# First attention logits of a graph network: every source lookup by TensorE, the sums by GpSimd

## The chip, the core and the metric

The kernel runs on one core of a Trainium2 chip. The metric is device time in microseconds for one launch, as a median over runs. The engines are TensorE (PE in the profile; PEld is its weight load), VectorE (DVE), ScalarE (ACT), GpSimd (POOL) and SyncE (SP). They run side by side and meet only at semaphores. GpSimd also issues the indirect DMAs, which fetch table rows by an index from memory.

## What is computed

Two graph attention layers, each with a residual and a layer norm, over 3125 nodes of 1024 numbers and 50000 edges. The change touches the first layer alone, and there only its logits:

```python
xp = (x @ W).reshape(N, H, C)                     # 3125 x 4 heads x 256
a_src = jnp.einsum('nhc,hc->nh', xp, att_src)     # 4 numbers a node
a_dst = jnp.einsum('nhc,hc->nh', xp, att_dst)
e = jax.nn.leaky_relu(a_src[src] + a_dst[dst], NEG_SLOPE)
m = jax.ops.segment_max(e, dst, num_segments=N)
ee = jnp.exp(e - m[dst])
z = jax.ops.segment_sum(ee, dst, num_segments=N)
out = jax.ops.segment_sum(xp[src] * (ee / z[dst])[:, :, None], dst, num_segments=N)
```

The edges are sorted by `dst`, and every node also has an edge to itself.

## The kernel before, in words

The sorted edges lie in chunks of 128, one edge on a partition: 391 chunks. The kernel walks windows of 64 destination nodes; a chunk that crosses a window's border is visited twice, so there are T = 440 steps. Four steps (U = 4) are a group, so there are NG = 110 groups of steps, and NGC = 98 groups of chunks. Five groups (GU = 5) are a unit; there are NU = 22 units.

A first block (to about 91 us of the profiled span) transposes x into `xT_all`, gets `a_src` and `a_dst` of all nodes (`a_all`), and builds the index tables. The block after it, here called the logits stage, does two things at once.

- **The product x @ W.** For each of 24 node tiles (the 25th is finished later) TensorE does 16 float32 matmuls of 512 columns (`products`, L990; a float32 matmul shows as two records in the trace). VectorE adds the bias and stores to `xp_st` (`evict_xp`, L1123), and SP writes it out. PSUM banks 0 to 3 hold two tiles.
- **The logits.** For each group TensorE fetches the destination part with a one-hot matrix of the local node number (`look_up`, L966, 4 matmuls), which VectorE has made by a comparison (`onehots`, L1072). VectorE adds the three bfloat16 parts (`reduce`, L1079). The source part `ga` comes in one of two ways. For groups 2 and 4 of each unit (`PICKS`, 38 of the 98 groups of chunks) VectorE compares the low 7 bits of the source number (`compare_sources`, L1100, and the tile number in L1103), TensorE multiplies the one-hot with the whole table (`look_up_sources`, L976, 12 matmuls of 100 columns, PSUM bank 6), and VectorE picks the right tile by a product and a sum (`pick_sources`, L1110 and L1114). For the other 60 groups (`FETCHED`) GpSimd issues four indirect DMAs each from `a_src_table` in device memory (`fetch_sources`, L165), and marks a landed group by a memset of one word (L383) that raises `s_fetched`. VectorE then adds the two parts (`logits`, L1089, 4 adds), copies the self part (L1092), and forms the slope (L1094).

The order is written out by hand, per unit. TensorE does `look_up`, in groups 1 and 3 `look_up_sources`, and then a slice of the product (4, 4, 4, 2, 2 matmuls after the five lookups). VectorE's `turn` for group g is: one-hot of g, reduction of g-1, logits of g-4 (LAG = 3). ScalarE's queue loads the rows `lt` and `low_bc`, broadcast to all partitions. `PoolGather.wait` sits between GpSimd's DMAs, and it goes two groups ahead of what has landed. When all logits are there (`s_lg`), TensorE transposes them (L1017), and the softmax scan starts. The later stages gather too: 440 rows of 4 KB for the first layer's sums, and 392 rows in the second layer's logits, all through L165.

Of the kernel before, what the change touches and what calls it, by code (L numbers as in the profile page):

```python
# [60 lines left out]
PICKS = (2, 4)  # L61
PICK_UNITS = NGC // GU
PICKED = [q for q in range(PICK_UNITS * GU) if q % GU in PICKS]
FETCHED = [q for q in range(NGC) if q not in PICKED]
NPICK = len(PICKED)
# [247 lines left out]
def gnn_kernel(nc, x, src, dst, w0, att_s, att_d, bias, rms_w, w_down, wl, wr, att1, w_up, out):  # L313
# [6 lines left out]
    as_t = nc.dram_tensor("a_src_table", (NP, H), F32, kind="Internal").ap()  # L320
# [16 lines left out]
    with top:  # L337
# [28 lines left out]
        chi = front.enter_context(nc.sbuf_tensor("chi", [P, NPICK, U], F32))  # L366
# [4 lines left out]
        s_ga = [sem(f"p1_ga{i}") for i in range(2)]  # L371
        s_fetched = sem("p1_fetched")
        EARLY = 1
        FIRST_K = 4

        def fetch_sources(pool, turns):
            gather = PoolGather(pool, N, bound)
            for p in turns:
                if p >= 2:
                    gather.wait(s_ga[p % 2], 64 * (p // 2))  # L380
                    q = FETCHED[p - 2]
                    gather.wait(s_fetched, q)
                    nc.gpsimd.memset(tick[:, q:q + 1], 0).then_inc(s_fetched, 2 if q + 1 in PICKED else 1)  # L383
                if p < len(FETCHED):
                    for c in range(FETCHED[p] * U, (FETCHED[p] + 1) * U):
                        gather.rows_of(ga[:, c, :], as_t, csrc[:, c:c + 1]).then_inc(s_ga[p % 2], 16)
            return gather
# [3 lines left out]
        with ExitStack() as ph:  # L391
# [83 lines left out]
            s_as = setup_sem("s_as")  # L475
# [74 lines left out]
            with nc.Block() as block:  # L550
                @block.gpsimd
                def _(pool):
                    pool.wait_ge(s_ct, 1)
                    pool.dma_start(edge_t.rearrange("(b p) n -> p b n", b=NB),
                                   ct[:].rearrange("p b f k -> p b (f k)")).then_inc(s_et, 16)
                    gather = PoolGather(pool, T, bound)
                    pool.wait_ge(s_ci, 1)
                    pool.wait_ge(s_et, 16)
                    for b in range(NB):
                        gather.rows_of(st[:, b, :, :].rearrange("p f k -> p (f k)"), edge_t, cii[:, b:b + 1])\  # L560
                              .then_inc(s_st, 16)
                    pool.wait_ge(s_csrc, 1)
                    pool.wait_ge(s_as, 32)
                    fetch_sources(pool, range(EARLY))

                @block.sync
                def _(sp):
# [29 lines left out]
                    as_rows = as_t.rearrange("(t p) h -> p t h", p=P)  # L597
                    with nc.allow_non_contiguous_dma(reason="four words a node"):
                        for i, tiles in enumerate((slice(0, HALF), slice(HALF, NT))):
                            sp.wait_ge(s_all, i + 1)  # L600
                            sp.dma_start(as_rows[:, tiles, :], a_all[:, tiles, 0:H]).then_inc(s_as, 16)
                    sp.wait_ge(s_et, 16)
                    sp.wait_ge(s_as, 32)
# [104 lines left out]
                def _(dve):  # L708
# [62 lines left out]
                    for n, i in enumerate(PICKS):  # L771
                        nc.vector.tensor_copy(chi[:, n::2, :], psum[:, 5, 0:PICK_UNITS * GU * U]
                                              .rearrange("p (q j) -> p q j", j=GU * U)[:, :, i * U:(i + 1) * U])
# [62 lines left out]
        with ExitStack() as ph:  # L836
# [8 lines left out]
            low_bc = sb("low_bc", [P, 2, U, P], BF16)  # L845
# [14 lines left out]
            s_low = [sem(f"p1_low{i}") for i in range(2)]  # L860
# [5 lines left out]
            s_hl = sem("p1_onehot_low")  # L866
            s_hp = sem("p1_looked_up")
# [18 lines left out]
            with nc.Block() as block:  # L886
                @block.gpsimd
                def _(pool):
                    fetch_sources(pool, range(EARLY, len(FETCHED) + 2))

# [14 lines left out]
                def _(act):  # L905
                    def load_low(u, n):
                        wait(act, s_hl, 2 * u + n - 1)
                        act.dma_start(low_bc[:, n].rearrange("p j e -> p (j e)"),
                                      low_t[bass.ds((GU * u + PICKS[n]) * U, U), :].rearrange("j e -> (j e)")
                                      .partition_broadcast(P)).then_inc(s_low[n], 16)  # L910
# [7 lines left out]
                    def unit(u, r, static):  # L918
                        for i in range(GU):
                            if i % 2 == 0 and i // 2 < 2 and static < PICK_UNITS:  # L920
                                load_low(u, i // 2)
                            load_lt(GU * u + i, i)
                    pairs(act, unit)
# [34 lines left out]
                def _(pe):  # L958
# [12 lines left out]
                    def look_up_sources(u, n):  # L971
                        pe.wait_ge(s_hl, 2 * u + n + 1)
                        wait(pe, s_hm, 2 * u + n)
                        for j in range(U):
                            for k in range(PARTS):
                                last = nc.tensor.matmul(psum[:, 6, j * NT * H:(j + 1) * NT * H], onehot_low[:, n, j, :],  # L976
                                                        as0[:, :, k, :], start=(k == 0), stop=(k == PARTS - 1))
                        last.then_inc(s_hp, 1)

                    def products(u, r, k0, k1):  # L980
                        if k0 == 0:
                            wait(pe, s_xe, u - 1)
                        for k in range(k0, k1):
                            for i in range(2):
                                if isinstance(u, int) and u == NT - 1:
                                    last = nc.tensor.matmul(
                                        psum[WN * i:WN * (i + 1), 2 * r], xT_all[:, u, k, 0:WN],
                                        w_sb[:, k, i * 512:(i + 1) * 512], start=(k == 0), stop=(k == KD - 1))
                                    continue
                                last = nc.tensor.matmul(  # L990
                                    psum[:, 2 * r + i], xT_all[:, u, k, :],
                                    w_sb[:, k, i * 512:(i + 1) * 512], start=(k == 0), stop=(k == KD - 1))
                        if k1 == KD:
                            last.then_inc(s_xp, 1)
# [7 lines left out]
                    SLICES = ((0, 2), (2, 4), (4, 6), (6, 7), (7, 8))  # L1002

                    def unit(u, r, static):
                        for i, (k0, k1) in enumerate(SLICES):
                            look_up(GU * u + i, i, (GU * r + i) % 2)
                            if i in (1, 3) and static < PICK_UNITS:
                                look_up_sources(u, i // 2)
                            products(u + 1, 1 - r, k0, k1)
# [53 lines left out]
                def _(dve):  # L1063
                    nc.vector.tensor_copy(w9[:, :, 2 * H], isfirst[:])
                    chunks = StepTiles(dve, ctab, "p1_c", U, NGC * U)
                    last_group = dve.alloc_register("p1_last")
                    group_of = dve.alloc_register("p1_last_bounded")

                    def onehots(g, i, s, m):
                        dve.wait_ge(s_lt[i], 16 * m + 16)  # L1070
# [5 lines left out]
                    def reduce(g, i, s):  # L1076
                        dve.wait_ge(s_pg, g + 1)
                        pv = psum[:, 4 + s, 0:U * PARTS * 2 * H].rearrange("p (j k n) -> p j n k", k=PARTS, n=2 * H)
                        nc.vector.tensor_reduce(out=at_dst[:, i], in_=pv, op=ALU.add, axis=AX.X).then_inc(s_at, 1)  # L1079

                    def logits(g, i, s, picks):
                        cs = chunks.load(g)
                        dve.reg_alu(last_group, chunks.regs[U - 1], 2, ALU.logical_shift_right)
                        dve.reg_alu(group_of, last_group, 0, ALU.max)
                        dve.wait_ge(s_at, g + 1)
                        wait(dve, s_hd, picks)
                        dve.wait_ge(s_fetched, dve.snap(group_of, min_val=0, max_val=NGC - 1) + 1)
                        for j in range(U):
                            last = nc.vector.tensor_tensor(esum[:, s, j], at_dst[:, i, j, 0:H],  # L1089
                                                           ga[:, bass.ds(cs[j], 1), :].rearrange("p a n -> p (a n)"), ALU.add)  # L1090
                        last.then_inc(s_es, 1)
                        nc.vector.tensor_copy(w9[:, bass.ds(g * U, U), H:2 * H], at_dst[:, i, :, H:2 * H])  # L1092
# [4 lines left out]
                    def compare_sources(u, n):  # L1097
                        dve.wait_ge(s_low[n], 16 * u + 16)
                        wait(dve, s_hp, 2 * u + n - 1)
                        nc.vector.tensor_scalar(onehot_low[:, n].rearrange("p j e -> p (j e)"),  # L1100
                                                low_bc[:, n].rearrange("p j e -> p (j e)"), pidx[:], None,
                                                ALU.is_equal).then_inc(s_hl, 1)
                        nc.vector.tensor_tensor(  # L1103
                            onehot_hi[:, n], bc(iotar[:, 0:NT].unsqueeze(1), [P, U, NT]),
                            bc(chi[:, bass.ds(2 * u + n, 1), :].rearrange("p a j -> p (a j)").unsqueeze(2), [P, U, NT]),
                            ALU.is_equal)

                    def pick_sources(u, n):
# [1228 lines left out]
```

## Time and profile before

| what | us |
|---|---|
| median of 3 runs | 2171.18 |
| lowest and highest run | 2164.91, 2173.71 |
| span of the profiled execution | 2761.9 |
| logits stage in that execution, first lookup to first transpose of the logits | 99.8 to 734.3 |
| GpSimd's last gather of `a_src` issued | 420.7 |

The profile is of one execution. It is to be read in this order: the span against the timed runs, the slices of engine activity, then the stretches 99 to 439 and 439 to 735 us apart, and inside each the list of instructions in order of time. In that list a row can stand for several instructions of one line (xN), and the bracket gives the idle time of the engine ahead of it and what ended it; "issue" means that nothing the profile shows was waited for.

### The profile page before, as it was taken

How to read it: one execution, taken by the hardware profiler on the slowest of the kernel's cores; microseconds unless marked ns; L12 is line 12 of the kernel's file. 1: busy time of each engine (PE TensorE's matmuls, PEld its weight loads, DVE VectorE, ACT ScalarE, POOL GpSimd, SP SyncE). 2: the span in 40 equal slices, each digit the busy share in tenths (PEclk: the TensorE clock that was granted, in tenths of full speed). 3: DMA queues.
4: the chain of work that ended last, by engine and by line, in shares of the span. 5: the costliest groups of instructions: out<-in, count | busy, mean ns of one | idle time of the engine just before them, and what ended most of it. 6: DMA issues, size and time to landing. Idle time of an engine off the chain costs nothing. (4 is left out here: it accounts for less than half of the span.)

```text
span 2761.9 us, 52467 instructions
## 1 busy us (share of the span) xinstructions
PE 1865.4 (68%) x11779; PEld 1216.8 (44%) x11780; DVE 1524.7 (55%) x4081; ACT 862.2 (31%) x2923; POOL 1346.7 (49%) x1446
## 2 busy tenths in 40 slices
PE   5612119999857777777774886367677676856678
PEld 4300004444434555545553775244445444545544
DVE  5301006777655555555555996254544544678878
ACT  3000000000246666656564674100000000046656
POOL 1576770000046666666663112826666666147781
PEclk9855558999979999999998998688888888979999
DMA  8201002332168888888887994556766666478857
GB/s 302 49 2 21 4 15 72 98 91 87 44 203 297 295 291 291 291 292 295 291 293 239 306 308 145 145 154 193 192 194 190 194 194 195 141 218 310 308 187 267
DMA packets 256917, 531.76 MB, mean 193 GB/s; under 512 B 50253, under 2 KB 148694, under 8 KB 256782
## 3 DMA queue, kind: packets, MB, share of 16 engines
q0 software_dynamic: 95376, 276.01, 32.0%
q1 hardware_dynamic: 124142, 220.58, 23.8%
q10 hardware_dynamic: 37296, 33.96, 5.0%
q8 instruction: 44, 0.72, 0.1%
q14 instruction: 59, 0.48, 0.1%
HBM read 441.14 MB, written 102.23 MB: 197 GB/s over the span
## 5 line engine op out<-in xcount | busy, mean ns | idle before, releaser
L165 POOL DMA_INDIRECT acc<-xl_table,csrc x392 | 401.3, 1024 | 243.7 <-issue 110.7
L1274 ACT ACTIVATE wone<-onehot,w 128x64 f32<-128x64 f32 x1760 | 433.3, 333 | 278.3 <-DVE onehot L1320 174.0
L1291 PE MATMUL banks<-w_sb,wone 128*64 128x256 f32 x2368 | 346.6, 416 | 135.1 <-DVE acc L1316 42.1
L990 PE MATMUL banks<-w_sb,acc 128*128 128x512 f32 x736 | 367.1, 637 | 36.7 <-issue 36.5
L1768 PE MATMUL banks<-xr_parts,onehot_t 128*128 x1320 | 228.3, 314 | 241.3 <-issue 186.4
L165 POOL DMA_INDIRECT w_sb<-xp_table,isrc x296 | 294.5, 995 | 171.8 <-PE banks L1294 91.5
L1808 DVE SCALAR_TENSOR_TENSOR prod<-banks,att_relu 128x1024 f32<-128x1024 f32 x110 | 134.6, 1223 | 323.2 <-ACT w L1727 238.2
L1316 DVE TENSOR_TENSOR acc<-banks,acc 128x512 f32 x440 | 304.4, 692 | 0.0
L1768 PEld LDWEIGHTS banks<-xr_parts,onehot_t 128*128 128x128 bf16 x1320 | 137.3, 104 | 343.7 <-issue 302.3
L165 POOL DMA_INDIRECT ga<-a_src_table,csrc x240 | 239.4, 998 | 94.9 <-issue 76.6
L1291 PEld LDWEIGHTS banks<-w_sb,wone 128*64 128x64 f32 x2368 | 183.1, 145 | 193.5 <-issue 83.2
L1773 PE MATMUL banks<-acc,ident 128*128 x880 | 259.1, 444 | 8.9 <-POOL tabs L1678 4.3
L1315 DVE TENSOR_TENSOR zacc<-banks,zacc 64x9 f32 x440 | 69.5, 158 | 319.0 <-PE banks L1294 198.8
L1727 ACT ACTIVATE w<-banks 128x32 f32 (+1 forms) x110 | 21.6, 197 | 664.8 <-remote 356.3
L990 PEld LDWEIGHTS banks<-w_sb,acc 128*128 128x128 f32 x736 | 137.2, 199 | 174.9 <-issue 174.8
L1773 PEld LDWEIGHTS banks<-acc,ident 128*128 128x128 f32 x880 | 186.7, 224 | 54.7 <-issue 16.0
L1079 DVE TENSOR_REDUCE at_dst<-banks 128x32 f32<-128x96 f32 x110 | 28.0, 255 | 330.9 <-remote 217.1
L1291 PE MATMUL banks<-rows_c,wone 128*64 128x256 f32 x1152 | 164.2, 414 | 63.6 <-ACT wone L1274 29.1
L926 ACT ACTIVATE zacc<-pidx 128x450 f32<-128x450 f32 x1 | 0.6, 578 | 620.1 <-DVE onehot_t L1072 620.1
L165 POOL DMA_INDIRECT rows_c<-xp_table,isrc x144 | 142.8, 992 | 89.3 <-PE banks L1294 53.7
L1918 POOL TENSOR_TENSOR msg<-rows,w 128x1536 f32<-128x1536 f32 x55 | 151.7, 2777 | 52.1 <-PE banks L1958 34.3
L1254 POOL MEMSET acc<- 128x3072 f32 x1 | 2.7, 2663 | 356.6 <-POOLq L886 356.6
(336 smaller groups left out, 2966.0 us busy)
## 6 DMA issues: line engine op xcount, KB each, us to landing
edge_rows<-acc SPq DMA_DIRECT2D x440, 130.0 KB
rows<-edge_rows SPq DMA_DIRECT2D x55, 1040.0 KB, 5.0
lt_bc<-local_dst ACTq DMA_DIRECT2D x110, 128.0 KB
lt<-local_dst ACTq DMA_DIRECT2D x110, 128.0 KB
w<-acc SPq DMA_DIRECT2D x100, 128.0 KB, 3.4
x_table<-y POOLq DMA_DIRECT2D x25, 512.0 KB, 6.2
acc<-x_table SPq DMA_DIRECT2D x25, 512.0 KB, 3.7
acc<-in_x SPq DMA_DIRECT2D x12, 1024.0 KB, 14.7
```

The lines of the kernel that those rows point to most:

```text
L165: return self.pool.indirect_dma_start(out, None, table, bass.IndirectOffsetOnAxis(ap=idx, axis=0), bounds_check=self.bound, oob_is_err=False)
L990: last = nc.tensor.matmul(psum[:, 2 * r + i], xT_all[:, u, k, :], w_sb[:, k, i * 512:(i + 1) * 512], start=(k == 0), stop=(k == KD - 1))
L1079: nc.vector.tensor_reduce(out=at_dst[:, i], in_=pv, op=ALU.add, axis=AX.X).then_inc(s_at, 1)
L1274: last = nc.scalar.activation(wone[:, s, j, h, :], onehot[:, s, j, :], ACT.Copy, scale=w9[:, bass.ds(g * U + j, 1), h:h + 1].rearrange("p ...
L1291: nc.tensor.matmul(psum[WN * a:WN * (a + 1), j, k * C:(k + 1) * C], wone[:, s, j, h, :], slots[r][:, j, h * C:(h + 1) * C], start=True, st ...
L1315: nc.vector.tensor_tensor(zv, psum[0:WN, 4 + j, 0:W9], zv, ALU.add)
L1316: nc.vector.tensor_tensor(av, psum[:, j, :], av, ALU.add).then_inc(s_acc, 1)
L1727: nc.scalar.activation(w9[:, bass.ds(g * U, U), 0:2 * H], psum[:, 4 * s2:4 * s2 + 4, HID:XRW], ACT.Copy).then_inc(s_sc, 1)
L1768: nc.tensor.matmul(psum[:, 4 * s2 + j, 0:XRW], onehot_t[:, s2, j, :], xr_parts[:, bass.ds(ds[j], 1), k, :].rearrange("p a n -> p (a n)"), ...
L1773: last = nc.tensor.matmul(psum[:, 4 * s2 + j, 0:XLW], ident[:], rows[:, bass.ds(ss[j], 1), :].rearrange("p a n -> p (a n)"), start=False, ...
L1808: nc.vector.scalar_tensor_tensor(out=prod[:, s], in0=psum[:, 4 * s:4 * s + 4, 0:HID], scalar=0.0, in1=bc(att_relu[:].unsqueeze(1), [P, U, ...
L1918: nc.gpsimd.tensor_tensor(msg[:, s, :, 0:POOL_HEADS, 0:HD], rows[:, r, :, 0:POOL_HEADS * HD].rearrange("p j (h c) -> p j h c", c=HD), bc(w ...
```

## The change

All 98 groups of chunks get their source part by `look_up_sources`, one in each group of steps; `fetch_sources`, `a_src_table`, its two stores and the marks are gone. The comparison result, the PSUM bank (6 + s) and `onehot_hi` are double buffered by s. `low_bc` is loaded for every group, five buffers deep, on the same semaphores as `lt`. The product's slices become 3, 3, 3, 3 and 4 matmuls. GpSimd runs a new loop, `sums`: the copy of the self part and the four adds; VectorE keeps only `slopes` of the logits.

```diff
-PICKS = (2, 4)
...
-    as_t = nc.dram_tensor("a_src_table", (NP, H), F32, kind="Internal").ap()
...
-        def fetch_sources(pool, turns):
...
-                    for c in range(FETCHED[p] * U, (FETCHED[p] + 1) * U):
-                        gather.rows_of(ga[:, c, :], as_t, csrc[:, c:c + 1]).then_inc(s_ga[p % 2], 16)
...
-                            sp.dma_start(as_rows[:, tiles, :], a_all[:, tiles, 0:H]).then_inc(s_as, 16)
...
-                    for n, i in enumerate(PICKS):
...
+                    nc.vector.tensor_copy(chi[:].rearrange("p q j -> p (q j)"), psum[:, 5, 0:NGC * U])
...
-                    fetch_sources(pool, range(EARLY, len(FETCHED) + 2))
+                    chunks = StepTiles(pool, ctab, "p1_c", U, NGC * U)
+
+                    def sums(g, i, s):
+                        cs = chunks.load(g)
+                        pool.wait_ge(s_at, g + 1)
+                        pool.wait_ge(s_hd, min(g + 1, NGC) if isinstance(g, int) else g + 1)
+                        wait(pool, s_lg, g - 1)
+                        nc.gpsimd.tensor_copy(w9[:, bass.ds(g * U, U), H:2 * H], at_dst[:, i, :, H:2 * H])
+                        for j in range(U):
+                            last = nc.gpsimd.tensor_tensor(esum[:, s, j], at_dst[:, i, j, 0:H],
+                                                           ga[:, bass.ds(cs[j], 1), :].rearrange("p a n -> p (a n)"), ALU.add)
+                        last.then_inc(s_es, 1)
...
                             load_lt(GU * u + i, i)
+                            if GU * static + i < NGC:
+                                load_low(GU * u + i, i)
...
+                    def look_up_sources(q, s):
+                        pe.wait_ge(s_hl, q + 1)
+                        wait(pe, s_hm, q - 1)
                         for j in range(U):
                             for k in range(PARTS):
-                                last = nc.tensor.matmul(psum[:, 6, j * NT * H:(j + 1) * NT * H], onehot_low[:, n, j, :],
+                                last = nc.tensor.matmul(psum[:, 6 + s, j * NT * H:(j + 1) * NT * H], onehot_low[:, s, j, :],
                                                         as0[:, :, k, :], start=(k == 0), stop=(k == PARTS - 1))
...
-                    SLICES = ((0, 2), (2, 4), (4, 6), (6, 7), (7, 8))
+                    SLICES = ((0, 3), (3, 6), (6, 9), (9, 12), (12, 16))
...
                     def reduce(g, i, s):
                         dve.wait_ge(s_pg, g + 1)
+                        wait(dve, s_es, g - (GU - 1))
...
-                    def logits(g, i, s, picks):
...
+                    def slopes(g, s):
                         dve.wait_ge(s_es, g + 1)
...
                         if not last:
-                            onehots(g, i, (GU * r + i) % 2, u)
...
+                            onehots(g, i, s, u)
+                        if first < NGC:
+                            compare_sources(g, i, s, u)
+                        if first >= 1 and not (last and i > 0):
+                            reduce(g - 1, (i - 1) % GU, s1)
+                        if 1 <= first <= NGC:
+                            pick_sources(g - 1, s1)
+                        if first >= 1 + LAG:
+                            slopes(g - 1 - LAG, (GU * r + i - 1 - LAG) % 2)
```

On TensorE, in the middle of a unit before, a group with a source lookup and the start of the next, which has none (`nt` is the table of destinations, `as` that of sources, ISA rows load registers):

```order
L966 MATMUL banks<-nt,onehot_t 128x24
L976 MATMUL banks<-as,onehot_low 128x100 x12
L990 MATMUL banks<-w_sb,acc 128x512 x2
L146 TENSOR_LOAD tabs
L147 ISA
L966 ISA
```

The same place now:

```order
L949 MATMUL banks<-nt,onehot_t 128x24
L959 MATMUL banks<-as,onehot_low 128x100 x12
L973 MATMUL banks<-w_sb,acc 128x512 x3
L142 TENSOR_LOAD tabs
L143 ISA
L949 ISA
```

The 12 matmuls now stand behind every lookup of destinations up to group 97, and the slice of the product behind them is 3 or 4 matmuls.

On VectorE, one turn of the second unit before, a turn without picks:

```order
L1072 TENSOR_SCALAR onehot_t<-lt_bc,pidx 128x512 [waits p1_pg,p1_lt1]
L1077 REGISTER_ALU
L1079 TENSOR_REDUCE at_dst<-banks 128x32 [waits p1_pg]
L146 ISA
L146 TENSOR_LOAD tabs
L147 ISA
L83 REGISTER_ALU [waits p1_at]
L1087 ISA [waits p1_picked]
L1089 ISA [waits p1_fetched]
L1089 TENSOR_TENSOR esum<-at_dst,ga 128x4
```

Every turn now, up to group 97 (`p1_es` is raised by GpSimd, `p1_looked_up` by TensorE):

```order
L1059 TENSOR_SCALAR onehot_t<-lt_bc,pidx 128x512 [waits p1_pg,p1_lt3]
L1077 TENSOR_SCALAR onehot_low<-low_bc,pidx 128x512 [waits p1_looked_up,p1_lt3]
L1080 ISA
L1080 TENSOR_TENSOR onehot_hi<-iotar,chi 128x100
L1067 TENSOR_REDUCE at_dst<-banks 128x32 [waits p1_es,p1_pg]
L1089 TENSOR_TENSOR picked<-banks,onehot_hi 128x400 [waits p1_looked_up,p1_picked,p1_onehot_hi]
L1093 ISA [waits p1_chosen]
L1093 TENSOR_REDUCE ga<-picked 128x16
L1071 ISA [waits p1_es]
L1071 SCALAR_TENSOR_TENSOR w<-esum 128x4x4
```

The register load, the four adds and the copy have left VectorE, and two comparisons, a product and a sum have come into each turn. On GpSimd the gathers give way to this row of work, here one group of steps:

```order
L142 TENSOR_LOAD tabs
L143 ISA
L863 COPY w<-at_dst 128x4x4
L865 ISA
L865 TENSOR_TENSOR esum<-at_dst,ga 128x4
L865 ISA
L865 TENSOR_TENSOR esum<-at_dst,ga 128x4
L865 ISA
L865 TENSOR_TENSOR esum<-at_dst,ga 128x4
L865 ISA
L865 TENSOR_TENSOR esum<-at_dst,ga 128x4
```

Before, four `L165 DMA ga<-a_src_table,csrc` and a one-word memset stood there for each of the 60 groups.

## Rows read from the trace of the kernel before

**Rows 1.** The page: span, and busy tenths of PE and GpSimd in 40 slices.

```profile
span 2761.9 us, 52467 instructions
...
PE   5612119999857777777774886367677676856678
...
POOL 1576770000046666666663112826666666147781
```

**Rows 2.** Busy us (and instructions) by stretch: PE, PEld, DVE, ACT, POOL, clock, DMA.

```profile
99.00:439.00 340.00, 88.91 (x262) 36.28 (x261) 35.23 (x141) 0.00 (x0) 235.78 (x290) 0.57 0.10 15
439.00:735.00 296.00, 294.79 (x1357) 140.95 (x1356) 203.51 (x913) 13.92 (x15) 0.00 (x0) 1.00 0.29 88
```

**Rows 3.** PE in order of time at 239 to 243 us: start, length, [idle before].

```profile
239.87 0.18 PE L966 MATMUL banks<-nt,onehot_t 128*128 x1 [1.79 <-issue]
242.68 0.18 PE L966 MATMUL banks<-nt,onehot_t 128*128 x1 [2.64 <-issue]
```

**Rows 4.** One unit of PE at 449 to 465 us, in order of time.

```profile
449.52 0.25 PE L966 MATMUL banks<-nt,onehot_t 128*128 x4
...
453.14 0.25 PE L966 MATMUL banks<-nt,onehot_t 128*128 x4
453.25 0.71 PE L976 MATMUL banks<-as,onehot_low 128*128 128x100 bf16 x12
...
457.30 0.25 PE L966 MATMUL banks<-nt,onehot_t 128*128 x4
...
465.26 0.25 PE L966 MATMUL banks<-nt,onehot_t 128*128 x4
```

**Rows 5.** GpSimd in order of time: one fetched group of four gathers, then the next.

```profile
274.77 0.99 POOL L165 DMA_INDIRECT ga<-a_src_table,csrc  x1 [0.22 <-issue]
...
279.97 1.00 POOL L165 DMA_INDIRECT ga<-a_src_table,csrc  x1 [0.21 <-issue]
```

**Rows 6.** L1808, once a group in the second layer's logits: busy us (count) by stretch.

```profile
1810.00:2360.00 550.00, 110.12 (x90) 0.86 0.68 191
2360.00:2430.00 70.00, 18.35 (x15) 0.95 0.34 102
```

**Rows 7.** GpSimd alone by L165 in three gathering stretches: busy us (count), clock, DMA.

```profile
99.90:420.00 320.10, 227.93 (x230) 0.56 0.09 12
800.00:1450.00 650.00, 403.80 (x407) 0.94 0.87 293
```

**Rows 8.** VectorE in order of time at 528 to 533 us.

```profile
528.52 0.35 DVE L1100 TENSOR_SCALAR onehot_low<-low_bc,pidx 128x512 bf16<-128x512 bf16 x1
528.79 0.25 DVE L1103 TENSOR_TENSOR onehot_hi<-iotar,chi 128x100 f32<-128x100 f32 x1
528.97 0.57 DVE L1110 TENSOR_TENSOR picked<-banks,onehot_hi 128x400 f32<-128x400 f32 x1
529.70 0.89 DVE L1114 TENSOR_REDUCE ga<-picked 128x400 f32 x1 [0.17 <-DVE picked L1110]
530.50 0.34 DVE L1072 TENSOR_SCALAR onehot_t<-lt_bc,pidx 128x512 bf16<-128x512 bf16 x1
530.76 0.25 DVE L1079 TENSOR_REDUCE at_dst<-banks 128x32 f32<-128x96 f32 x1
...
531.69 0.18 DVE L1094 SCALAR_TENSOR_TENSOR w<-esum 128x16 f32 x1
531.87 1.23 DVE L1123 TENSOR_TENSOR xp_st<-banks,bias_bc 128x1024 f32<-128x1024 f32 x1
```

**Rows 9.** GpSimd's computing instructions elsewhere in the program, in order of time.

```profile
6.00 0.19 POOL L508 CAST step<-stepi 110x4 f32<-110x4 int32 x1
...
6.87 0.30 POOL L514 CAST pidx<-tabs 128x1 f32<-128x1 int32 x1
```

**Rows 10.** The end of the logits stage in order of time.

```profile
728.84 0.55 DVE L1089 TENSOR_TENSOR esum<-at_dst,ga 128x4 f32<-128x4 f32 x4 [0.68 <-DVE at_dst L1079]
...
734.33 1.90 PE L1017 MATMUL banks<-ident,w 128*110 128x128 f32 x15 [1.21 <-DVE w L1094]
```

More of the change, by code:

```diff
@@ L888, in _, with unit @@
                 def _(pool):
-                    fetch_sources(pool, range(EARLY, len(FETCHED) + 2))
+                    chunks = StepTiles(pool, ctab, "p1_c", U, NGC * U)
[9 more added lines that the diff above has]
+                        last.then_inc(s_es, 1)
+                    def unit(u, r, static):
+                        for i in range(GU):
+                            sums(GU * u + i, i, (GU * r + i) % 2)
+                    pairs(pool, unit)
                 @block.sync
@@ L977, in look_up_sources, with halves @@
                                                         as0[:, :, k, :], start=(k == 0), stop=(k == PARTS - 1))
                         last.then_inc(s_hp, 1)
-                    def products(u, r, k0, k1):
[L981 to L994, printed above, removed]
+                    def halves(u, r, n0, n1):
+                        if n0 == 0:
+                            wait(pe, s_xe, u - 1)
+                        for n in range(n0, n1):
+                            k, i = divmod(n, 2)
+                            if isinstance(u, int) and u == NT - 1:
+                                last = nc.tensor.matmul(
+                                    psum[WN * i:WN * (i + 1), 2 * r], xT_all[:, u, k, 0:WN],
+                                    w_sb[:, k, i * 512:(i + 1) * 512], start=(k == 0), stop=(k == KD - 1))
+                                continue
+                            last = nc.tensor.matmul(
+                                psum[:, 2 * r + i], xT_all[:, u, k, :],
+                                w_sb[:, k, i * 512:(i + 1) * 512], start=(k == 0), stop=(k == KD - 1))
+                        if n1 == 2 * KD:
+                            last.then_inc(s_xp, 1)
@@ L1095, in logits, with compare_sources @@
                                                        in1=esum[:, s], op0=ALU.mult, op1=ALU.max).then_inc(s_lg, 1)
[L1097 to L1101, printed above, removed]
+                    def compare_sources(q, i, s, m):
+                        dve.wait_ge(s_lt[i], loaded(i, m))
+                        wait(dve, s_hp, q - 1)
+                        nc.vector.tensor_scalar(onehot_low[:, s].rearrange("p j e -> p (j e)"),
+                                                low_bc[:, i].rearrange("p j e -> p (j e)"), pidx[:], None,
@@ L1124, in evict_xp, with turn @@
                                                 bias_bc[:], ALU.add).then_inc(s_xe, 1)
[L1126 to L1127 removed]
+                    def turn(u, r, i, static):
+                        g, first, last = GU * u + i, GU * static + i, static == NU
+                        s, s1 = (GU * r + i) % 2, (GU * r + i - 1) % 2
                         if not last:
[L1129 to L1137 removed]
+                            onehots(g, i, s, u)
[7 more added lines that the diff above has]
+                            slopes(g - 1 - LAG, (GU * r + i - 1 - LAG) % 2)
                     def unit(u, r, static):
@@ L1156, in _ @@
                         for r in range(2):
-                            unit(2 * pair + r, r, 0)
+                            unit(2 * pair + r, r, 2)
                     for u in range(2 * (PICK_UNITS // 2), NU):
@@ L1160, in _ @@
                     for i in range(LAG + 1):
[L1161 removed]
+                        turn(NU, NU % 2, i, NU)
                         if i == 1:
```

114 lines of the change are left out of this document (29 added, 85 removed).

## Prediction, written before the run

> **What bounds the kernel now.** I read first the span against the timed runs, because they differ more than the change could move. The profiled span is 2761.9 us [rows 1], the median 2171.18 us, so 591 us of the profiled execution are in no timed run. A sum made against this profile is worth nothing before it is known whose 591 us they are. So the second view is the busy slices: the logits stage lies in slices 2 to 11 of 69 us each; in slices 3 to 6 GpSimd is at 6 or 7 tenths and PE at 1 or 2, in slices 7 to 10 PE is at 9 and GpSimd at 0 [rows 1]. Taken by itself this reads as "the gathers of a_src hold TensorE up for 340 us, take them away". The stretches say the same in sums: from 99 to 439 us PE is busy 89 of 340 us at a mean granted clock of 0.57, with 236 us of GpSimd; from 439 to 735 it is busy 295 of 296 us at full clock, with none [rows 2].
>
> The third view, instructions in order of time, speaks against that reading. Between 239 and 243 us PE runs the single matmuls of one lookup, with only a register instruction between them, and each stands 2.81 us behind the one before, idle "issue" 2.64 us [rows 3]. At 453.14 us four of the same kind fit in 0.25 us [rows 4]. No semaphore stands between these four, so a gather that isn't back can't be what they wait for. A gather can hold VectorE's logits, and through the buffers a lookup, but not the second matmul of four. Nor do the gathers come late: GpSimd's four of a group take 279.97 - 274.77 = 5.20 us [rows 5], 3 groups in 5 are fetched, so it feeds a unit of five groups each 15.6 us, and a unit of PE takes 465.26 - 449.52 = 15.74 us [rows 4]. It starts ahead of PE, and 110 groups of steps need only 98 groups of chunks. What I see there is engines slowed in their issue while small gathers are in flight, in this profiled execution.
>
> Are these stalls in the timed runs too? The bookkeeping says no. Without them the stage's 22 units would be 19 with two source lookups at 15.74 us and 3 without. A source lookup costs PE (457.30 - 453.14) - (453.14 - 449.52) = 4.16 - 3.62 = 0.54 us [rows 4], so a unit without is 15.74 - 1.08 = 14.66 us. Sum: 19 x 15.74 + 3 x 14.66 = 343 us, against 630 us in the profile (99.8 us to about 729.4): **287 us lost**. The second layer's logits, under gathers too, take 550 / 90 = 6.11 us a group and, once the gathers have ended, 70 / 15 = 4.67 us [rows 6]; 1.44 us by some 98 groups is 141 us. The gathers for the first layer's sums come each 650 / 407 = 1.60 us [rows 7] where GpSimd alone needs 1.30 [rows 5]; 0.30 by 440 is 132 us. Together 560 us, near the 591 to be explained. If the 287 us were real in timed runs, 591 us would have to come from what gives 273. So I take it that **in the timed runs the stage is bound by TensorE already**, at about 343 us, and that the gathers run hidden beside it.
>
> **The change part by part.**
>
> *TensorE.* 60 more source lookups by 0.54 us = 32.4 us, on the engine that sets the end; the matmuls of the product and the lookups of destinations are the same in number. A unit with five lookups is 14.66 + 5 x 0.54 = 17.36 us, 3.47 us a group. The new slices only spread this more evenly. Sum for the stage: 343 + 32 = 375 us.
>
> *GpSimd's gathers and the a_src_table.* 240 gathers by 1.30 us go, 312 us of GpSimd, hidden beside 343 us of TensorE: worth 0 in the timed runs. Their cover is thin. Before would be gather bound if one took over (99.8 + 343 - 8 - 92) / 236 = 1.45 us, with 92 us where the stage's gathers start, 236 of them, and some 8 us from the last landing to the stage's end. The rows give 1.30 alone and 320.1 / 230 = 1.39 with all waits [rows 5, 7]; the 1.60 of the later stage is the far bound, and there GpSimd also waits for TensorE and 4 KB rows. At 1.60 the old stage would be 35 us longer, and the change worth -3 us instead of +32. I take 1.30 to 1.39, since these are the same gathers. The two stores of a_src_table end beside VectorE's table building: 0.
>
> *VectorE.* From start to start [rows 8]: comparison 0.27, tile comparison 0.18, product 0.73, sum 0.80, one-hot 0.26, reduction 0.25, slope 0.18: 2.67 us a group, and 1.23 us of eviction a unit, 5 x 2.67 + 1.23 = 14.6 us. That fits under 17.36 us of TensorE, with 2.8 us left in a unit. Order matters as well: TensorE's next lookup needs one-hot and comparison, which stand behind product and sum of the group before. From the end of a source lookup these are 0.73 + 0.80 + 0.18 + 0.26 + 0.27 = 2.2 us, and TensorE has its slice (2.6 us), the next lookups (0.6 us) and one more slice in hand before it needs them. So no wait.
>
> *GpSimd's sums.* Five small instructions and a register load a group. None like them stands in the trace. A small conversion takes 0.19 to 0.30 us [rows 9], VectorE's gap for the same register load and waits is 0.68 us [rows 10]. 5 x 0.19 + 0.68 = 1.6 us at the low end, 5 x 0.30 + 0.68 = 2.2 us at the high one; it speaks in the end only from 3.47 us a group on. LAG of three turns, some 10 us, hides the way from VectorE to GpSimd and back. What is queued behind it: VectorE's slope, and behind that the next one-hots. 0 us.
>
> *DMAs.* low_bc is loaded 98 times instead of 38, 128 KB each: 10 loads of 128 KB in 17.4 us, 75 GB/s, five buffers ahead. 0 us. *Ends.* The first block's copy to chi is longer, +0.2 us. At the end TensorE waited 1.21 us for the last slope [rows 10]; now a slice of 4 matmuls stands behind the last lookup, and VectorE's four late logits are only four slopes: -1.2 us.
>
> Sum: +32.4 + 0.2 - 1.2 = +31.4 us, and **2171.2 + 31.4 = 2202.6 us**, 1.4% slower. Against the profile's own time the sum is another: the stage loses 630 - 343 = 287 us of stalls with the gathers and gains 31, so I expect a profiled span of about 2761.9 - 287 + 31 = 2506 us, if the stalls elsewhere stay. The profiled execution should look 256 us faster while the median is 31 us slower.
>
> **A rule of the skill.** The comparisons treat 128 x 512 bfloat16 in 0.35 us [rows 8], over one element a nanosecond on each partition, and GpSimd has computed next to nothing beside them in this stage. The Trainium skill ("SBUF — State Buffer", Who interferes with whom) says that VectorE in a two-port mode, or with two SBUF inputs against a GpSimd instruction that reads SBUF, shares a port pair with GpSimd as a lock, and the later one blocks fully. By that rule the sums given to GpSimd are paid back in part by VectorE's comparisons, and the change comes out slower yet: it is the mechanism of rival (c), which is priced below from rows. No row of this trace has small GpSimd sums beside such comparisons, so it shows neither.
>
> **The rivals.** (a) *The stalls are real*, and the gathers hold the timed runs too, wholly or in part. For it: they are long and in the trace, and the change's gain in the profile is large. Against: the bookkeeping. In full 2171 - 256 = 1915 us; at a third of it about 2107. Chance 0.13. (b) *Gathers a little slower* than in the rows: at a cadence of 1.50 us the old stage is 236 x (1.50 - 1.45) = 11 us over TensorE's sum, at 1.65 us 47 us, so the new time is 2171 + 31 - 11 = 2191 to 2171 + 31 - 47 = 2155 us. For it: 15.6 against 15.7 us a unit, and 1.60 in rows 7. Against: 1.30 stands wherever GpSimd isn't waiting. Chance 0.14: 0.03 faster, 0.08 within 0.5% of before, 0.03 slower. (c) *VectorE becomes the bound* on account of GpSimd's instructions: each of the five holds VectorE up for its own length, 5 x (0.19 to 0.30) = 0.95 to 1.5 us a group. VectorE is then at 14.6 / 5 + 0.95 = 3.87 to 4.4 us a group against TensorE's 3.47: 98 groups by 0.4 to 0.95 = 39 to 93 us more, 2242 to 2296 us. It decides from 0.55 us a group on. Chance 0.12. (d) *GpSimd is the bound*, over 3.47 us a group, through waits and register work that cost more than on VectorE; at 4 us a group 98 x 0.5 = 52 us, 2255 us. Chance 0.04.
>
> **How the numbers follow.** The forecast as worked out, 2190 to 2215 us, has 0.57. With it, of rival (b) what lies above 2165 us, 0.12, and of (c) and (d) the cheaper part, 0.10, make 0.79; so the range is **2165 to 2260 us**. About 0.5% (11 us) is what a measurement of this kernel can tell from no change. Slower by more: 0.57 + 0.12 + 0.04 + 0.03 = 0.76. Within: 0.08. Faster: 0.13 + 0.03 = 0.16.
>
> **What would show it.** In the profile after: PE busy over 95% of the logits stage from its first unit, a unit each 17.4 us, the stage from about 99.8 to 475 us, granted clock near 1.0 all through, no rows of single matmuls 2 us apart. A group with a wait on PE for the comparison or the sum speaks for (c), longer comparisons beside GpSimd's adds too; VectorE idle ahead of L1071 for GpSimd speaks for (d). If the profiled span falls by some 250 us and the median falls too, step one of this prediction, whose the 591 us are, was wrong.

## The result, and the profile after

| | median us | runs | lowest to highest |
|---|---|---|---|
| before | 2169.89 | 4 | 2164.91 to 2173.71 |
| after | 2205.31 | 4 | 2204.37 to 2206.15 |

The changed kernel takes 1.0165 times as long as the one before, 95% interval [1.0151, 1.0179], so it is **35 us slower**. The 2171.18 us ahead of the prediction is the median of three of the four runs. The profile shown there is of a disturbed execution, 591 us longer than that median, and no other profile shown here is like it. The profile after has a span of 2201.9 us, 2.5 us less than the time of its own run (2204.37 us), so here profile and median speak of the same thing.

The page of the profile after: span, and busy tenths in 40 slices of 55 us (PE, GpSimd, granted clock).

```profile
span 2201.9 us, 54102 instructions
...
PE   4899999995888888888849884777777777466688
...
POOL 1122222213777777777711117777777776588780
PEclk9999999997999999999979996999999999699999
```

The answer to [rows 1]: PE is at 9 from the third slice to the ninth, the end of the stage, with no valley in it, and GpSimd is at 2 where it had 6 or 7. The same view in numbers, with the columns of [rows 2] (PE, PEld, DVE, ACT, POOL busy, then clock, DMA share, GB/s):

```profile
101.00:439.00 338.00, 338.00 (x2194) 179.81 (x2193) 260.69 (x699) 0.00 (x0) 88.38 (x480) 1.00 0.43 105
```

TensorE is busy for all of 338 us, at full clock; GpSimd for 88. VectorE has 261 of 338 us, 77%. One unit of PE in order of time, lookups of destinations and one source lookup, the answer to [rows 4]:

```profile
239.54 0.25 PE L949 MATMUL banks<-nt,onehot_t 128*128 x4
...
242.83 0.25 PE L949 MATMUL banks<-nt,onehot_t 128*128 x4
242.93 0.71 PE L959 MATMUL banks<-as,onehot_low 128*128 128x100 bf16 x12
243.48 2.80 PE L973 MATMUL banks<-w_sb,acc 128*128 128x512 f32 x6
...
256.84 0.25 PE L949 MATMUL banks<-nt,onehot_t 128*128 x4
```

A unit takes 256.84 - 239.54 = 17.30 us, forecast 17.36. From the start of the 12 matmuls to that of the product behind them 0.55 us pass, forecast 0.54 a lookup. Who waited, from 95 to 480 us (engine, line, what for, total us, times, longest):

```profile
POOL w L863 <- DVE w L1071: 268.4, 107, 5.7
...
DVE at_dst L1067 <- PE banks L949: 62.4, 73, 3.6
DVE picked L1089 <- PE banks L959: 30.0, 78, 0.4
...
DVE at_dst L1067 <- POOL esum L865: 0.5, 1, 0.5
```

VectorE waits for TensorE and GpSimd for VectorE; nobody waits for GpSimd but once, for 0.5 us, and no wait of PE for VectorE or GpSimd is in the list of which these are four rows. The stage is bound by TensorE.

### The profile page after: what moved, and what is told of

It is laid out like the page before. It is cut to its first block and busy times, and to the rows that moved or that the text cites. A ratio compares the mean times of both kernels' runs of the same rounds, so it can differ in the third digit from the quotient of the medians.

```text
span 2201.9 us, 54102 instructions
## 1 busy us (share of the span) xinstructions
PE 1766.9 (80%) x12499; PEld 1188.3 (54%) x12500; DVE 1564.3 (71%) x3770; ACT 861.0 (39%) x2923; POOL 1208.2 (55%) x1697
## 5 line engine op out<-in xcount | busy, mean ns | idle before, releaser
L1265 PE MATMUL banks<-w_sb,wone 128*64 128x256 f32 x2368 | 316.0, 392 | 78.1 <-DMA w_sb<-xp_table,isrc 48.9
L973 PE MATMUL banks<-w_sb,acc 128*128 128x512 f32 x736 | 342.7, 605 | 0.0
L1742 PE MATMUL banks<-xr_parts,onehot_t 128*128 x1320 | 189.7, 288 | 133.4 <-issue 94.9
L1747 PE MATMUL banks<-acc,ident 128*128 x880 | 226.9, 402 | 7.4 <-POOL tabs L1652 7.2
L1265 PEld LDWEIGHTS banks<-w_sb,wone 128*64 128x64 f32 x2368 | 161.6, 137 | 127.8 <-issue 47.4
L863 POOL COPY w<-at_dst 128x16 f32 (+1 forms) x110 | 30.3, 276 | 307.8 <-DVE w L1071 268.4
L1747 PEld LDWEIGHTS banks<-acc,ident 128*128 128x128 f32 x880 | 162.4, 195 | 44.0 <-issue 10.4
L1932 PE MATMUL banks<-msg,acc 128*64 128x132 f32 x1760 | 126.8, 287 | 62.9 <-DVE acc L1961 32.6
L1268 PEld LDWEIGHTS banks<-w,onehot 128*64 128x64 f32 x880 | 120.9, 137 | 64.3 <-issue 0.8
L1932 PEld LDWEIGHTS banks<-msg,acc 128*64 128x64 f32 x1760 | 100.2, 138 | 89.6 <-issue 38.4
```

Of the source, the lines that this page charges most:

```text
L973: last = nc.tensor.matmul(psum[:, 2 * r + i], xT_all[:, u, k, :], w_sb[:, k, i * 512:(i + 1) * 512], start=(k == 0), stop=(k == KD - 1))
L1265: nc.tensor.matmul(psum[WN * a:WN * (a + 1), j, k * C:(k + 1) * C], wone[:, s, j, h, :], slots[r][:, j, h * C:(h + 1) * C], start=True, st ...
L1268: nc.tensor.matmul(psum[0:WN, 4 + j, 0:W9], onehot[:, s, j, :], w9[:, bass.ds(i, 1), :].rearrange("p a n -> p (a n)"), start=True, stop=Tr ...
L1742: nc.tensor.matmul(psum[:, 4 * s2 + j, 0:XRW], onehot_t[:, s2, j, :], xr_parts[:, bass.ds(ds[j], 1), k, :].rearrange("p a n -> p (a n)"), ...
L1747: last = nc.tensor.matmul(psum[:, 4 * s2 + j, 0:XLW], ident[:], rows[:, bass.ds(ss[j], 1), :].rearrange("p a n -> p (a n)"), start=False, ...
L1932: last = nc.tensor.matmul(psum[WN * a:WN * (a + 1), bank, c:c + 2 * HS], onehot[:, u, first + j, :], msg[:, s, j, 2 * a:2 * a + 2, :].rear ...
```

## The experiments

### The kernel before, profiled again

No edit.

> The kernel before, once more with a profile. Theory A (the 591 us by which the profiled span of before exceeds its timed runs belong to that one execution, and no stall of them is in the kernel's own time): time 2170 us, profiled span about 2167 us, logits stage from about 100 to 442 us, TensorE busy in it all through, a unit each 15.7 us, gathers 1.30 us apart in every stage, and from this profile to the changed kernel's the stage grows by 31 to 36 us. Rival B (a profile always slows the engines while the small gathers of a_src are in flight): time 2170 us, span again about 2760 us with single matmuls some 2 us apart.

Measured: 2169.69 us, ratio 1.0003 [0.9992, 1.0013]; span 2170.5 us. Theory A held, B fell. The stretch of the gathers in this profile, with the columns of [rows 2]:

```profile
102.00:409.00 307.00, 307.00 (x1471) 148.39 (x1470) 220.72 (x930) 0.00 (x0) 236.20 (x287) 1.00 0.38 93
```

PE in order of time inside that stretch, one unit:

```profile
301.76 0.25 PE L966 MATMUL banks<-nt,onehot_t 128*128 x4
301.86 0.71 PE L976 MATMUL banks<-as,onehot_low 128*128 128x100 bf16 x12
302.41 1.94 PE L990 MATMUL banks<-w_sb,acc 128*128 128x512 f32 x4
...
317.49 0.25 PE L966 MATMUL banks<-nt,onehot_t 128*128 x4
```

TensorE is busy for 307 of 307 us while GpSimd is busy for 236 of them: both at once, where [rows 2] had 89 of 340. A unit is 317.49 - 301.76 = 15.73 us, as in the second half of the disturbed profile [rows 4]. Three more lookups make it 17.30 us in the changed kernel: 1.57 us, 0.52 us a lookup. This is the profile that the one after must be set against. The first lookup and the first transpose of the logits here, in PE's order of time:

```profile
101.56 0.25 PE L966 MATMUL banks<-nt,onehot_t 128*128 x4
...
449.31 2.00 PE L1017 MATMUL banks<-ident,w 128*110 128x128 f32 x16 [1.21 <-DVE w L1094]
```

The same two rows of the profile after:

```profile
101.04 0.25 PE L949 MATMUL banks<-nt,onehot_t 128*128 x4
...
479.00 1.91 PE L1003 MATMUL banks<-ident,w 128*110 128x128 f32 x16
```

From the first lookup to the first transpose of the logits: 449.31 - 101.56 = 347.8 us before, 479.00 - 101.04 = 378.0 us after, **30.2 us more**. The 1.21 us of waiting for the last slope are gone, as in the sum. Behind the stage the two executions take 2170.5 - 449.31 = 1721.2 and 2201.9 - 479.00 = 1722.9 us. The stalls of [rows 3], and the slower later stages too, are absent: while the first layer's rows are gathered the page's slices show 354 to 365 GB/s, where the disturbed one had 291 to 297.

### The kernel before, without gathers

The 60 groups take zeros for their source part, so this kernel leaves a part of the logits out.

```diff
-                    gather.wait(s_ga[p % 2], 64 * (p // 2))
...
-                if p < len(FETCHED):
-                    for c in range(FETCHED[p] * U, (FETCHED[p] + 1) * U):
-                        gather.rows_of(ga[:, c, :], as_t, csrc[:, c:c + 1]).then_inc(s_ga[p % 2], 16)
...
-                    fetch_sources(pool, range(EARLY))
+                    nc.gpsimd.memset(ga[:], 0.0)
```

> The kernel before without its 240 gathers of a_src: the 60 groups take zeros for their source part, so that part of the logits is left out; the marks stay, so no engine waits for the gathers. Theory A (the gathers are wholly hidden by TensorE's products): 2168 to 2171 us, ratio 0.998 to 1.001. Rival C (the gathers hold the stage in part, by their cadence of 1.30 to 1.39 us): 2155 us or less. Rival B (profiling and small gathers): time 2170 us but a profiled span of 2170 us as well, where before had 2762.

Measured: 2170.94 us, ratio 1.0013 [1.0002, 1.0023]. Taking all 240 gathers away gains nothing; they are hidden. This is the result that says what the change could not win.

### Source lookups twice

```diff
-                        for j in range(U):
+                        for j in (*range(U), *range(U)):
                             for k in range(PARTS):
                                 last = nc.tensor.matmul(psum[:, 6 + s, j * NT * H:(j + 1) * NT * H], onehot_low[:, s, j, :],
```

> The changed kernel with every source lookup done twice (24 matmuls of 100 columns for 12, the same result written again). Theory (TensorE sets the end of the stage, 0.54 us a lookup): 98 x 0.54 = 53 us, about 2258 us. Rival (the 35 us of the change come from VectorE or GpSimd, with TensorE having room): 2205 to 2225 us.

Measured: 2254.51 us, ratio to before 1.0397 [1.0377, 1.0416], 49.2 us over the changed kernel. PE in order of time in this run, from first lookup to first transpose:

```profile
98.22 0.25 PE L949 MATMUL banks<-nt,onehot_t 128*128 x4
...
530.06 1.91 PE L1003 MATMUL banks<-ident,w 128*110 128x128 f32 x16
```

431.8 us, 53.9 more than after, by 98 lookups 0.55 us each. (The first lookup starts 2.8 us earlier here, so the time grew by less than the stage.) The price of a lookup is paid in full, so TensorE is the bound; 60 lookups of this price are 33 us, nearly all that the change costs.

### The sums back on VectorE

```diff
-                    pairs(pool, unit)
+                    pass
...
-                    def slopes(g, s):
+                    chunks = StepTiles(dve, ctab, "p1_c", U, NGC * U)
+
+                    def slopes(g, i, s):
+                        cs = chunks.load(g)
+                        dve.wait_ge(s_at, g + 1)
+                        dve.wait_ge(s_hd, min(g + 1, NGC) if isinstance(g, int) else g + 1)
+                        for j in range(U):
+                            last = nc.vector.tensor_tensor(esum[:, s, j], at_dst[:, i, j, 0:H],
+                                                           ga[:, bass.ds(cs[j], 1), :].rearrange("p a n -> p (a n)"), ALU.add)
+                        last.then_inc(s_es, 1)
+                        nc.vector.tensor_copy(w9[:, bass.ds(g * U, U), H:2 * H], at_dst[:, i, :, H:2 * H])
```

> The changed kernel with one half undone: all source lookups by TensorE, but the sums and the copy of the self part by VectorE, GpSimd idle. Theory (VectorE's work per group decides once it passes TensorE's 3.47 us): VectorE has 2.67 us + a fifth of 1.23 + some 0.68 of register load, 0.53 of adds and 0.16 of copy = 4.3 us a group, so 98 x 0.83 = 81 us over the changed kernel, about 2286 us. Rival (VectorE's idle share of the changed kernel swallows the sums, so that the move to GpSimd is worth nothing): 2205 us. Rival (GpSimd's instructions hold VectorE up by the shared port, so without them VectorE gains): under 2245 us.

Measured: 2211.68 us, ratio to before 1.0193 [1.0176, 1.021], 6.4 us over the changed kernel, where 81 were expected. Neither the theory's size nor the rival's zero is right. VectorE in order of time, one turn:

```profile
243.97 0.56 DVE L1060 TENSOR_TENSOR esum<-at_dst,ga 128x4 f32<-128x4 f32 x4
244.52 0.17 DVE L1063 COPY w<-at_dst 128x16 f32 x1
244.67 0.17 DVE L1065 SCALAR_TENSOR_TENSOR w<-esum 128x16 f32 x1
244.78 0.35 DVE L1043 TENSOR_SCALAR onehot_t<-lt_bc,pidx 128x512 bf16<-128x512 bf16 x1
...
247.23 0.56 DVE L1060 TENSOR_TENSOR esum<-at_dst,ga 128x4 f32<-128x4 f32 x4
```

A turn is 247.23 - 243.97 = 3.26 us, where I had 4.0 without the eviction. Most of the difference is the 0.68 us of register load that I took from [rows 10] as a cost of each group. Ahead of the adds, which stand behind that load, VectorE is idle in this run for 0.01 us (median) in the 95 places where the source sum of 0.87 us comes just before. In the second profile of before, where in most groups the short reduction (0.25 us) comes just before, the mean idle time is 0.77 us in the 36 places where that reduction had itself waited for TensorE, and 0.36 us in the 71 others. So the load costs little where a longer instruction stands ahead of it.

With the eviction VectorE has 5 x 3.26 + 1.2 = 17.5 us a unit by this sum against TensorE's 17.3. Measured, the first two units take 17.3 us and those from the fourth to the seventeenth 18.1 to 18.4, so VectorE is the bound by some 0.9 us a unit. TensorE is no longer fed at every lookup: the four matmuls of a lookup of destinations take 0.56 us at 249.68 us and 0.49 us at 253.37 us, where they take 0.25 in a full stream.

From first lookup (100.37 us) to first transpose (491.47 us) the stage takes 391.1 us, 13 more than after; the time grew by half of that. The profiled spans show where the rest went: 0.7 us ahead of the stage and 5.2 us behind it, 3.0 of these from the first to the last matmul of the first layer's weighted sums (572.8 us here, 575.8 after). In all three profiled executions in which GpSimd adds the logits this part takes 575.0 to 575.8 us, in the six profiled executions of the other kernels, the disturbed one apart, 571.5 to 572.8; why stays open. GpSimd's part of the change is thus worth 13 us in the stage and some 6 us in time; the intervals of the two ratios touch, though the runs of the two kernels lie apart (2204.37 to 2206.15 and 2207.92 to 2213.33 us).

### GpSimd's adds twice

```diff
+            spare = sb("spare", [P, 2, U, H])
...
                         for j in range(U):
+                            nc.gpsimd.tensor_tensor(spare[:, s, j], at_dst[:, i, j, 0:H],
+                                                    ga[:, bass.ds(cs[j], 1), :].rearrange("p a n -> p (a n)"), ALU.add)
+                        for j in range(U):
                             last = nc.gpsimd.tensor_tensor(esum[:, s, j], at_dst[:, i, j, 0:H],
```

> The changed kernel with GpSimd's four adds done twice a group (once more into a spare tile), so 9 small instructions for 5. In the changed kernel the four adds take 0.65 us and GpSimd idles 2.2 to 3.2 us a group. Theory (GpSimd's sums are hidden, and its instructions don't hold VectorE up): 2205 us, within 0.2% of the changed kernel, the comparisons on VectorE at 0.35 us as before. Rival (the shared port: each of GpSimd's instructions holds VectorE up for its length, and VectorE's room is 2.8 us a unit): 20 more adds a unit by 0.2 us = 4 us of holding, over the room by 1.2 us, 22 x 1.2 = 26 us more, about 2231 us.

Measured: 2203.77 us, ratio to before 1.0163 [1.0148, 1.0179]; its runs (2201.02 to 2206.09 us) take in all of the changed kernel's. The theory held, the port rival fell. GpSimd and VectorE side by side in that run:

```profile
246.13 0.35 DVE L1063 TENSOR_SCALAR onehot_t<-lt_bc,pidx 128x512 bf16<-128x512 bf16 x1
246.39 0.35 DVE L1081 TENSOR_SCALAR onehot_low<-low_bc,pidx 128x512 bf16<-128x512 bf16 x1
246.48 0.49 POOL L864 COPY w<-at_dst 128x16 f32 x1 [1.62 <-DVE w L1075]
246.65 0.26 DVE L1084 TENSOR_TENSOR onehot_hi<-iotar,chi 128x100 f32<-128x100 f32 x1
```

The comparisons stand 0.26 us apart, as in [rows 8], while the copy takes 0.49 us. The profile after has the case beside which it is to be read:

```profile
245.63 0.34 DVE L1059 TENSOR_SCALAR onehot_t<-lt_bc,pidx 128x512 bf16<-128x512 bf16 x1
245.88 0.20 POOL L863 COPY w<-at_dst 128x16 f32 x1 [2.60 <-DVE w L1071]
245.89 0.34 DVE L1077 TENSOR_SCALAR onehot_low<-low_bc,pidx 128x512 bf16<-128x512 bf16 x1
246.15 0.25 DVE L1080 TENSOR_TENSOR onehot_hi<-iotar,chi 128x100 f32<-128x100 f32 x1
```

Here the copy runs beside the two bfloat16 comparisons alone, and takes 0.20 us. What it must not meet is the tile comparison behind them (L1080, L1084 in the run above), the one of the three that combines two tensors (`pidx` is one number a partition). Of the 110 copies of the profile after, the 48 that overlap it take 0.32 to 0.49 us and the next GpSimd instruction starts 0.28 to 0.45 us behind them; the 62 others, 37 of them beside the bfloat16 comparisons, take 0.19 to 0.20 us, and the next starts 0.15 to 0.17 us behind. The tile comparison takes 0.25 us either way. So there is an interference, it is with this one instruction, and it is GpSimd's small instruction that pays, although it started first.

### A fifth gather in each group

```diff
-        ga = front.enter_context(nc.sbuf_tensor("ga", [P, NGC * U, H], F32))
+        ga = front.enter_context(nc.sbuf_tensor("ga", [P, NGC * U + 2, H], F32))
...
-                    gather.wait(s_ga[p % 2], 64 * (p // 2))
+                    gather.wait(s_ga[p % 2], 80 * (p // 2))
...
+                    gather.rows_of(ga[:, NGC * U + p % 2, :], as_t, csrc[:, c:c + 1]).then_inc(s_ga[p % 2], 16)
```

> The kernel before with a fifth gather in each of the 60 fetched groups (one row set twice, into a spare column). Theory (the gathers are hidden as long as GpSimd keeps up, which ends at 1.45 us a gather of four, 5.8 us a group): five gathers of 1.30 us are 6.5 us a group, 59 x 6.5 = 384 us from 92 us on, and some 8 us behind the last: the stage ends at 484 instead of 443 to 449 us, so 2169 + 35 to 41 = 2204 to 2210 us. Rival (gathers run fully beside everything, their cadence isn't what the stage needs): 2169 us.

Measured: 2203.76 us, ratio 1.016 [1.0145, 1.0176], 34.2 us over before. Who waited in this run's stage (engine, line, what for, total us, times, longest):

```profile
DVE esum L1090 <- POOL tabs L383: 74.0, 40, 5.2
```

The last mark of GpSimd and the first transpose behind it, in order of time:

```profile
479.76 0.09 POOL L383 MEMSET tabs<- 1x1 int32 x1 [2.74 <-DMA ga<-a_src_table,csrc]
...
480.82 3.67 PE L1018 MATMUL banks<-ident,w 128*110 128x128 f32 x16 [9.33 <-DVE w L1095]
```

With a quarter more of them the gathers are the bound: VectorE waits 74 us in 40 places for the mark of a landed group, and TensorE 9.33 us at the end. So the cover was thin, as the prediction said: 1.63 us for each gather that is used is over what the stage allows (1.45 us by the sum), and the 1.30 us of the old split, two groups on TensorE and three on GpSimd, under it.

### A version that beats both

```diff
-PICK_UNITS = NGC // GU
+PICK_UNITS = 17
```

> The kernel before with source lookups by TensorE in 17 units instead of 19 (34 groups instead of 38), the other 64 groups gathered. Theory (TensorE sets the end at 0.54 us a lookup, and gathers have room up to 64 groups): -4 x 0.54 = -2.2 us, 2167 us; the gathers' end moves from 409 to about 430 us. Rival (the room of GpSimd is used up already, since its last gather came at 409 us and not at 399): 2170 to 2180 us.

Measured: 2166.87 us, ratio 0.9991 [0.9982, 1.0]. The stage runs from 100.80 to 446.53 us, 345.7 us against 347.8: 2.0 us less for four lookups less, as expected, but as a time it is at the edge of what can be told apart. With it, and two bfloat16 parts for three in the source lookups, which keeps less of `a_src` (some 16 bits):

```diff
-                            for k in range(PARTS):
+                            for k in range(2):
...
-                                                        as0[:, :, k, :], start=(k == 0), stop=(k == PARTS - 1))
+                                                        as0[:, :, k, :], start=(k == 0), stop=(k == 1))
```

> As the one with 17 units, and each source lookup of TensorE sums two bfloat16 parts of a_src instead of three (8 matmuls for 12), which rounds a_src to some 16 bits. Theory (TensorE sets the end; a third of a lookup is 0.18 us): 34 x 0.18 = 6 us less than that one, about 2161 us. Rival (with TensorE faster the gathers become the bound: GpSimd's last group at 430 us and 8 us behind it against TensorE's 443 - 2 - 6 = 435 us): the gain stops at 3 us, 2164 to 2168 us.

Measured: 2161.55 us, ratio 0.9965 [0.9951, 0.9979]: 8 us faster than before, 44 us faster than the changed kernel. PE in order of time in this run, first lookup and first transpose:

```profile
99.57 0.25 PE L966 MATMUL banks<-nt,onehot_t 128*128 x4
...
439.17 2.00 PE L1017 MATMUL banks<-ident,w 128*110 128x128 f32 x16 [1.55 <-DVE w L1094]
```

339.6 us for the stage, 8.1 less than before. The way that pays is the opposite of the change's: less work for the lookups on TensorE, and more gathers on GpSimd while they stay covered. Of the 8 us, 5 to 6 are bought with the precision of `a_src`; what more gathers alone give is the 2 to 3 us of the run before it.

## Why the prediction was right, and where it was not

- **Whose the 591 us are.** This step carried the forecast. Read alone, [rows 1] and [rows 2] promise a gain of 256 us. The matmuls 2.8 us apart with nothing to wait for [rows 3] said that something not in the program slowed the engines, and the sum of the excess in the gathering stretches (560 of 591 us) said that timed runs have none of it. The second profile of before shows it. The argument was thinner than it looked, though. Of the 251 us that PE is idle from 99 to 439 us, six single gaps of 10 to 53 us make 191, and each stands ahead of the first matmul of a lookup, where PE does wait for semaphores; in them VectorE stands still too, while GpSimd goes on with its gathers. The argument from matmuls without a semaphore between them covers only part of the other 60 us, and the rest was carried by the bookkeeping, which the second profile bears out. And I tied the stalls to the small gathers being in flight, in that execution; no run bears that out: the profile of the same kernel again has none of them, nor has the one with a fifth gather in each group. What slowed that one execution stays open; no run here reproduces it.
- **The profiled span after.** Forecast 2506 us "if the stalls elsewhere stay", measured 2201.9. The condition failed, since stalls of a disturbed execution don't carry over to another one. The forecast for the timed run did not rest on it.
- **TensorE: 60 x 0.54 = 32.4 us.** Measured 0.55 a lookup in the rows after and for the doubled lookups, and 0.52 as what three more of them add to a unit. 60 x 1.57 / 3 = 31.4, less 1.2 at the end, is the 30.2 us by which the stage grew, against 31.2 in the sum (32.4 - 1.2).
- **Gathers worth nothing.** Right: without them the ratio is 1.0013. The break-even of 1.45 us a gather was somewhat low. With the fifth gather, 1.63 us per useful one, the formula gives 42 us, and 34.2 were measured. The last gather starts at 475.9 us there and the transpose at 480.8, so 5 us stand behind it and not 8; with that and the stage's end at 449.3 the break-even is about 1.49 us, an estimate.
- **VectorE 2.67 us a group, no wait.** Right in the trace: no wait of PE for it. By the rule on the shared port (the Trainium skill, "SBUF — State Buffer", Who interferes with whom) a VectorE instruction with two SBUF inputs contends with a GpSimd instruction that reads SBUF, and whichever comes later is blocked. The trace agrees on the pair (the copy of 0.20 us takes up to 0.49 beside the tile comparison, which reads two tensors) and not on the order: there the copy started first and was the one to grow. Beside the bfloat16 comparisons alone neither side grew. Rival (c) thus had its victim the wrong way round: VectorE's comparisons keep 0.346 us, and doubling GpSimd's adds costs nothing.
- **GpSimd 1.6 to 2.2 us a group.** The four adds take 0.65 us together and the copy 0.20, or more beside the tile comparison; busy time is 88.38 us for 96 groups, 0.92 us each. It idled ahead of nearly every copy, 268 us in all for VectorE's slope, so whatever the register load costs lies inside that idle time.
- **The size.** 31.4 us forecast, 35.4 measured. The two profiled spans differ by 31.4 us: 30.2 in the stage, 1.7 behind it, and 0.5 less ahead of it. The sum's term of 31.2 us is thus 1 us too large for the stage. From 31.4 to 35.4 the two profiled runs lead: before's took 2172.17 us, 2.3 above the median of 2169.89, after's 2204.37 us, 0.9 below its median, and the time outside the span is 0.8 us longer after. So the forecast of 31.4 us and the 31.4 us between the spans agree by chance: a term 1 us too large stands against 1.2 us outside the stage that no term gave. In absolute terms the stage takes 347.8 and 378.0 us, where the sum had 343 and 375; the 3 to 5 us missing in both fall out of the difference.

## What to carry to other kernels

Before any stretch of a profile is read, set its span against the timed runs; where it is far longer, find stalls between instructions that have no semaphore between them, add up what is lost in every stretch, and take the profile again. An engine that is busy 77% of the time beside a full one was hidden here, and work taken from it was worth nothing, while the same work given to the full engine cost its whole price. A split of work between two engines is best judged by what each has left at the end of the stage, and tried one group at a time.

## What was not expected of the hardware

- One execution of 2761.9 us in a kernel whose timed runs lie within 2164 to 2174: matmuls of one lookup 2.1 to 2.8 us apart and six gaps of 10 to 53 us, with granted clock 0.57 in that stretch, and no cause that the trace names.
- A register load ahead of VectorE's adds that shows as a gap of 0.77 us in the mean behind a reduction that had waited shows as 0.01 us (median) behind a sum of 0.87 us.
- Beside VectorE's float32 tile comparison, 128x100 with two input tensors, a small GpSimd copy that started first grows from 0.20 to between 0.32 and 0.49 us, and the comparison doesn't grow; beside bfloat16 comparisons of one 128x512 tensor with a number a partition the copy stays at 0.20 us.
